# Causal attention inside a two-layer block: head pairs on 32-row quarters, values as weights on four 32-column quarters

## The reference, cut to what matters

```python
# causal attention of layer 1, per batch of 512 tokens
qkv = (x @ Wqkv).reshape(b, t, 3, H, HD)          # H = 8 heads, HD = 16
scores = q @ k.T * scale + head_scales * geo_bias # the bias is folded into Wqkv's q part
scores = where(causal, scores, -inf)
attn = softmax(scores)
out = attn @ v                                    # then @ Wout, times the gate, + x
```

## Time and profile before

| what | value |
|---|---|
| median of 3 runs (2993.34 to 3004.03) | 2995.16 us |
| the profiled execution | 2994.33 us |
| its span, first to last instruction | 2992.5 us |
| mean granted TensorE clock | 0.929 of full speed |
| PE / DVE / ACT / POOL busy | 84% / 52% / 46% / 27% |
| scores of the causal attention (L888), start of the first 128-key and of the first 512-key one, batch alone | 195.4 and 228.6 us |
| the same, first batch beside running heads | 449.1 and 496.2 us |
| starts of that block in the next five batches | 797.9, 1149.4, 1501.8, 1852.5, 2200.7 us |

### The profile page before, as it was taken

The page is one execution under the profiler, slowest core; times in us unless marked ns, Lnnn a source line. Parts: engine busy times, 40 slices in busy tenths (PEclk is TensorE's granted clock), DMA queues, the critical chain, the costliest instruction groups (busy, mean ns, idle before and its releaser), DMA issues. The chain is left out here.

```text
span 2992.5 us, 45343 instructions
## 1 busy us (share of the span) xinstructions
PE 2503.9 (84%) x15660; PEld 1542.3 (52%) x15660; DVE 1556.1 (52%) x2640; ACT 1361.7 (46%) x2923; POOL 802.5 (27%) x376
## 2 busy tenths in 40 slices
PE   4886899889897898889898898978988898976676
PEld 2354347544565546654465445754456544753454
DVE  4224673547536483455735475364834557347432
ACT  0232236462455525563364624645255633643354
POOL 1001650018301290014600174011910147015200
PEclk6886899999899998999899998999989999998798
DMA  2110110103010120112101030101201121000111
GB/s 76 42 50 1 33 39 8 51 15 89 2 43 15 43 62 2 43 29 57 34 1 57 15 79 12 43 15 43 61 2 43 29 57 33 15 19 15 23 29 33
DMA packets 210740, 101.70 MB, mean 34 GB/s; under 512 B 137367, under 2 KB 189620, under 8 KB 210492
## 3 DMA queue, kind: packets, MB, share of 16 engines
q1 hardware_dynamic: 205052, 95.74, 11.4%
q10 hardware_dynamic: 5440, 2.75, 0.3%
HBM read 77.48 MB, written 20.99 MB: 33 GB/s over the span
## 5 line engine op out<-in xcount | busy, mean ns | idle before, releaser
L721 POOL TENSOR_TENSOR prod<-pv,mixv 128x1024 f32<-128x1024 f32 x190 | 610.5, 3257 | 251.9 <-ACT pv L1179 172.7
L1561 DVE TENSOR_REDUCE nmax<-bank 128x1 f32<-128x512 f32 x512 | 341.1, 687 | 595.2 <-PE bank L1015 592.8
L1218 ACT ACTIVATE prT<-bank 128x512 f32<-128x512 f32 x512 | 305.7, 597 | 624.5 <-PE bank L736 620.9
L1015 PE MATMUL bank<-keys,qs 64*128 64x512 f32 x896 | 279.6, 702 | 191.6 <-ACT pr L1231 61.5
L660 POOL TENSOR_TENSOR rstd<-vareps,minus_half 128x4 f32<-128x4 f32 x48 | 48.5, 1010 | 1288.7 <-DVE vareps L1325 1288.7
L1231 ACT ACTIVATE pr<-bank,nmax 128x512 f32<-128x512 f32 x512 | 349.9, 686 | 82.4 <-DVE nmax L1561 81.0
L736 PE MATMUL bank<-ident,pr 128*128 128x128 f32 x2048 | 353.5, 299 | 35.5 <-ACT prT L1218 35.5
L736 PEld LDWEIGHTS bank<-ident,pr 128*128 128x128 f32 x2048 | 243.2, 151 | 269.2 <-issue 216.6
L1119 ACT ACTIVATE arena<-bank 128x512 f32<-128x512 f32 x256 | 152.9, 597 | 473.0 <-PE bank L848 423.0
L1052 PE MATMUL bank<-prT,vals 128*64 128x128 f32 x3584 | 264.5, 293 | 47.5 <-ACT prT L1218 47.5
L1523 DVE TENSOR_REDUCE vals<-prod 128x128 f32<-128x1024 f32 x224 | 269.3, 1209 | 42.5 <-POOL prod L721 42.5
(11 more groups left out here) (231 smaller groups left out, 3274.2 us busy)
## 6 DMA issues: line engine op xcount, KB each, us to landing
Wg<-in_L_ffn_Wg SPq DMA_DIRECT2D x64, 256.0 KB, 2.7
Wu<-in_L_ffn_Wu SPq DMA_DIRECT2D x64, 256.0 KB, 3.1
Wd<-in_L_ffn_Wd SPq DMA_DIRECT2D x64, 256.0 KB, 3.8
out_rows<-on SPq DMA_DIRECT2D x32, 512.0 KB, 2.6
onR<-out_rows SPq DMA_DIRECT2D x32, 512.0 KB, 3.8
xin<-in_L_attn_x SPq DMA_DIRECT2D x8, 256.0 KB, 4.0
mask_rows<-masko SPq DMA_DIRECT2D x8, 256.0 KB, 4.3
maskR<-mask_rows SPq DMA_DIRECT2D x8, 256.0 KB, 6.6
```

The costliest lines, as they stand in the source:

```text
L721: g.tensor_tensor(*value_piece(n), ALU.mult).then_inc(vprod_r[0], 1)
L1015: pe.matmul((S0, S1)[(turn + odd) % 2][:, :], qs[half, j % 3, r, :], keys[half, p, :], start=True, stop=True).then_inc(s_ps[0], 1)
L1218: s.activation(prT[:, m % 3, :], TB[:, :], ACT.Copy).then_inc(pT_r[0], 1)
L1561: v.tensor_reduce(nmax[:, m % 2:m % 2 + 1], (S0, S1)[turn % 2][:, :], X_AXIS, ALU.max, negate=True).then_inc(nmax_r[0], 1)
```

## The change

The causal attention's matmuls are cut to tiles of the array, and what is weight and what is streamed is swapped in the value product.

- Masked keys: instead of eight copies, `k1z` has two (`[2, T]`): heads of even number kept, or heads of odd number kept. DVE makes both straight from PSUM. The copies on ACT and POOL are gone.
- Scores: two heads of a pair are issued together at even steps, each on its own 32 rows of the array (a 32-row quarter holds an even and an odd head; the mask of the copy blanks the other). The order of heads is `ORDER1`, so that a pair lies on two different quarters. Both wait for the exp of the head before, because both banks F0 and F2 are written.
- `p1` has four buffers, `p1T` six, `nmax1` four columns.
- Value product: `v1` (padded to 32 columns) is the weight on one of four 32-column quarters, `p1T` is streamed, four heads (`QUAD`) at a time at steps n % 4 == 2. It comes out transposed, ACT copies it to `o1T`, two transposes bring it back, and DVE copies as before.
- The stage has two more marks (`E1`).

```diff
-E1 = A1 + N1 + 3
+E1 = A1 + N1 + 5
+ORDER1 = (0, 2, 1, 3, 4, 6, 5, 7)
+QUAD = 4
+DV = 32
+NPT = 6
...
-        k1z = part(0, [H1, T])
-        v1 = sb("v1", [P, NT, H1, D1 + 1])
-        nmax1 = sb("nmax1", [P, 2])
-        p1 = part(4096, [2, T])
-        p1T = part(5120, [2, T])
+        k1z = part(0, [2, T])
+        v1 = sb("v1", [P, NT, H1, DV])
+        o1T = sb("o1T", [P, 2 * P])
+        nmax1 = sb("nmax1", [P, 4])
+        p1 = part(1024, [4, T])
+        p1T = part(3072, [NPT, T])
...
-                wait(g, k1_r, b, 1)
-                for h in range(H1 // 2, H1):
-                    g.tensor_tensor(k1z[:, h, :], k1T, head_of16[:, h:h + 1].to_broadcast([P, T]), ALU.mult).then_inc(k1z_r[1][0], 1)
...
-                for n in range(N1 + 3):
-                    if n < N1:
-                        i, h = n // H1, n % H1
+                wait(pe, k1_r, b, 2)
+                for n in range(N1 + 5):
+                    if n < N1 and n % 2 == 0:
+                        i = n // H1
                         w = (i + 1) * P
-                        f = (F0, F2)[n % 2]
-                        if i == 0:
-                            wait(pe, k1z_r[h // (H1 // 2)], b, h % (H1 // 2) + 1)
-                        if n >= 2:
-                            wait(pe, p1_r, b, n - 1)
-                        pe.matmul(f[:, 0:w], q1T[:, i * P:(i + 1) * P], k1z[:, h, 0:w], start=True, stop=False, skip_group_check=True)
-                        pe.matmul(f[:, w - P:w], ident_bf[:, :], causal_bf[:, :], start=False, stop=True, skip_group_check=True).then_inc(s1_ps[0], 1)
+                        wait(pe, p1_r, b, n)
+                        for odd, f in enumerate((F0, F2)):
+                            h = ORDER1[n % H1 + odd]
+                            rows = slice(h // 2 * 2 * D1, h // 2 * 2 * D1 + 2 * D1)
+                            pe.matmul(f[:, 0:w], q1T[rows, i * P:(i + 1) * P], k1z[rows, h % 2, 0:w], start=True, stop=False, skip_group_check=True)
+                        for f in (F0, F2):
+                            pe.matmul(f[:, w - P:w], ident_bf[:, :], causal_bf[:, :], start=False, stop=True, skip_group_check=True).then_inc(s1_ps[0], 1)
...
-                    if n >= 3:
+                    if 3 <= n <= N1 + 2 and n % QUAD == (QUAD + 2) % QUAD:
...
                         for j in range(i + 1):
-                            last = pe.matmul(F1[:, h * (D1 + 1):(h + 1) * (D1 + 1)], p1T[:, m % 2, j * P:(j + 1) * P], v1[:, j, h, :], start=(j == 0), stop=(j == i))
+                            for k in range(QUAD):
+                                h = ORDER1[QUAD * half + k]
+                                c = h % QUAD * DV
+                                last = pe.matmul(F1[c:c + DV, half * P:(half + 1) * P], v1[:, j, h, :], p1T[:, (m - QUAD + 1 + k) % NPT, j * P:(j + 1) * P], start=(j == 0), stop=(j == i), skip_group_check=True)
...
+                    if n >= H1 + 4 and n % H1 == 4:
+                        i = n // H1 - 1
+                        wait(pe, o1T_r, b, i + 1)
+                        for half in range(2):
+                            last = pe.transpose(F1[:, (2 + half) * P:(3 + half) * P], o1T[:, half * P:(half + 1) * P], ident[:, :])
+                        last.then_inc(o1_ps[0], 1)
...
-                for h in range(H1 // 2):
-                    s.activation(k1z[:, h, :], k1T, ACT.Copy, scale=head_of16[:, h:h + 1]).then_inc(k1z_r[0][0], 1)
...
+                    if n >= H1 + 3 and n % H1 == 3:
+                        i = n // H1 - 1
+                        wait(s, o1T_ps, b, 2 * i + 2)
+                        s.activation(o1T[:, :], F1[:, 0:2 * P], ACT.Copy).then_inc(o1T_r[0], 1)
...
-                v.tensor_copy(k1T, F2[:, :]).then_inc(k1_r[0], 1)
+                for odd in range(2):
+                    v.tensor_scalar(k1z[:, odd, :], F2[:, :], parity[:, odd:odd + 1], None, ALU.mult).then_inc(k1_r[0], 1)
```

More of the change, by code:

```diff
@@ L359, in build @@
         p1T_r = sem("p1T_r", N1)
+        o1T_ps = sem("o1T_ps", 2 * NT)
+        o1T_r = sem("o1T_r", NT)
         o1_ps = sem("o1_ps", NT)
@@ L895, in attn1 @@
                             wait(pe, p1T_r, b, m)
-                        transposes(F3, lambda j: p1[:, m % 2, j * P:(j + 1) * P], i + 1).then_inc(p1_T[0], 1)
-                    if n >= 3:
+                        transposes(F3, lambda j: p1[:, m % 4, j * P:(j + 1) * P], i + 1).then_inc(p1_T[0], 1)
+                    if 3 <= n <= N1 + 2 and n % QUAD == (QUAD + 2) % QUAD:
                         m = n - 3
-                        i, h = m // H1, m % H1
-                        if h == 0 and i >= 1:
+                        i, half = m // H1, m % H1 // QUAD
+                        if half == 0 and i >= 1:
                             wait(pe, o1_r, b, i)
@@ L1140, in attn1 @@
                         wait(s, p1_T, b, m + 1)
-                        s.activation(p1T[:, m % 2, 0:w], F3[:, 0:w], ACT.Copy).then_inc(p1T_r[0], 1)
+                        if m >= NPT:
+                            wait(s, o1T_ps, b, (m - NPT) // QUAD + 1)
+                        s.activation(p1T[:, m % NPT, 0:w], F3[:, 0:w], ACT.Copy).then_inc(p1T_r[0], 1)
                     if n < N1:
@@ L1144, in attn1 @@
                         wait(s, nmax1_r, b, n + 1)
-                        if n >= 2:
-                            wait(s, p1_T, b, n - 1)
-                        s.activation(p1[:, n % 2, 0:w], (F0, F2)[n % 2][:, 0:w], ACT.Exp, bias=nmax1[:, n % 2:n % 2 + 1]).then_inc(p1_r[0], 1)
+                        if n >= 4:
+                            wait(s, p1_T, b, n - 3)
+                        s.activation(p1[:, n % 4, 0:w], (F0, F2)[n % 2][:, 0:w], ACT.Exp, bias=nmax1[:, n % 4:n % 4 + 1]).then_inc(p1_r[0], 1)
                     yield A1 + 1 + n
@@ L1429, in attn1 @@
                 wait(v, qkv1_ps, b, 2)
-                v.tensor_copy(k1T, F2[:, :]).then_inc(k1_r[0], 1)
+                for odd in range(2):
+                    v.tensor_scalar(k1z[:, odd, :], F2[:, :], parity[:, odd:odd + 1], None, ALU.mult).then_inc(k1_r[0], 1)
                 yield A1
-                for n in range(N1 + 3):
-                    if n >= H1 + 3 and n % H1 == 3:
+                back = F1[:, 2 * P:4 * P].rearrange("p (h e) -> p h e", e=DV)[:, :, 0:D1 + 1]
+                for n in range(N1 + 5):
+                    if n >= H1 + 5 and n % H1 == 5:
                         i = n // H1 - 1
                         wait(v, o1_ps, b, i + 1)
-                        v.tensor_copy(o1[:, i, :, :].rearrange("p h d -> p (h d)"), F1[:, 0:H1 * (D1 + 1)]).then_inc(o1_r[0], 1)
+                        v.tensor_copy(o1[:, i, :, :], back).then_inc(o1_r[0], 1)
                     if n < N1:
@@ L1439, in attn1 @@
                         wait(v, s1_ps, b, n + 1)
-                        if n >= 2:
-                            wait(v, p1_r, b, n - 1)
-                        v.tensor_reduce(nmax1[:, n % 2:n % 2 + 1], (F0, F2)[n % 2][:, 0:w], X_AXIS, ALU.max, negate=True).then_inc(nmax1_r[0], 1)
+                        if n >= 4:
+                            wait(v, p1_r, b, n - 3)
+                        v.tensor_reduce(nmax1[:, n % 4:n % 4 + 1], (F0, F2)[n % 2][:, 0:w], X_AXIS, ALU.max, negate=True).then_inc(nmax1_r[0], 1)
                     yield A1 + 1 + n
                 wait(v, o1_ps, b, NT)
-                v.tensor_copy(o1[:, NT - 1, :, :].rearrange("p h d -> p (h d)"), F1[:, 0:H1 * (D1 + 1)]).then_inc(o1_r[0], 1)
+                v.tensor_copy(o1[:, NT - 1, :, :], back).then_inc(o1_r[0], 1)
                 wait(v, o1_r, b, NT)
```

15 lines of the change are left out of this document (7 added, 8 removed).

## The result

The change takes 3080.18 us (median of 4 runs, 3070.89 to 3081.10) against 2994.25 (4 runs, 2988.66 to 3004.03): ratio 1.0279, interval 1.0258 to 1.0299. That is 86 us slower where 13 were predicted, and outside the range. The profiled execution has a span of 3078.7 us.

What follows compares the result with a forecast made beforehand. TensorE was taken to bound the causal-attention block. 2994.3 us plus 3.5 for seven batches beside running heads (+0.5 each) plus 9 for the batch alone gave 3007 us; 8-in-10 range 2960 to 3050.

Steps and rivals of the forecast that it cites:

- PE's saving, 12.7 us a batch: Causal attention's tiled scores and value products take 32.3 us of PE per batch instead of 45.0, saving 12.7.
- that rival: Value products: four column tiles overlap only two by two, 4.4 us more per batch, 3042 us; chance 0.10.
- Masked keys, 1.7 us: Dropping ACT's masked key copies lets the running head's max and exp start earlier: 1.7 us gained per batch.
- New waits, 15.8 us more a batch: Score pairs beside running heads wait longer, mainly for exps: 18.8 us per batch, replacing 3.0 of old waits.
- "I take +0.5" a batch: Net per batch beside running heads: sum +1.4, lowered to +0.5 because waits were charged in full; 3.5 us for seven.
- The two more marks: Two more steps at the end of the stage, priced in the batch alone: about 1.3 us.
- The batch alone, +9: The batch without running heads gets slower: pairs +6.4, end steps 1.3, copies -1.5, clock 0 to 8; +9 in all.
- the clock's term: In the batch alone, PE about half busy lowers the granted clock: 0 to 8 us more.
- My check for this batch: The batch alone should take 57 to 68 us in the next profile instead of 53.
- The slower rival: Running heads' copies and exps delay odd heads' exps on ACT at most pairs: 3041 us, range 3021 to 3075; chance 0.22.

Runs made afterwards that it cites:

- products: Kernel before with the change's column-tiled value products, head order and two marks; whole-array single scores and eight key copies as before: 2977.39 us, ratio 0.9928.
- order: The change with transposes, products and transposes back written ahead of the score pair in each step, same instructions: 3051.12 us, ratio 1.0186.
- pair: The change with its score pairs on the whole array and eight masked key copies instead of 32-row tiles and two copies: 3111.96 us, ratio 1.0377.
- spread: The change with only its table of weights altered, so a running-head step stands ahead of each pair: 2921.38 us, ratio 0.9728.
- filler: The change plus ten unread mask products on PE ahead of 10 of the 15 later score pairs per batch: 3051.05 us, ratio 1.0183.
- spread, filler: The spread kernel plus ten unread mask products ahead of 10 of the 15 later score pairs, in the batch alone only: 2913.13 us, ratio 0.9738.

## Why the prediction was wrong, point by point

- **PE's saving, 12.7 us a batch: right in kind, 2.3 too small.** It is 15.0 by the account. A quad of value products shows 32 instructions from 507.21 to a modelled end 1.08 us later (*products*), eight waves of 0.11 and 0.20 around them, so four column tiles overlap as two do and that rival falls. Two 32-row scores start 0.007 us apart.
- **Masked keys, 1.7 us: right.** The 2.77 us wait of the earlier trace rows is 1.00 us, and two copies instead of eight gave 15 us in all.
- **New waits, 15.8 us more a batch: right.** 14.9 by the account, 17.1 instead of 3.0 in the profile's list of the block, L1162 as releaser. `o1T`'s copy releases nobody for long, and the transposes back do not stand in that list.
- **"I take +0.5" a batch: the step that failed.** I let PE's rate stand at full clock through seven blocks that I had just filled with waits, and charged the clock (0 to 8 us) only to the batch alone. It cost 13.0 us a batch, 11.7 of them inside the block. From the second batch's first score to the last batch's, six batches on, the program takes 2093.2 us before and 2167.6 after, +74.4 where I had +3.0; this is nearly all of the error of 73. Not all of the loss is the new waits': 2.8 of the 11.7 us come with the two marks alone, and pairs on the whole array lose 5.7 less than the same pairs on row tiles. The row that should have warned was mine: the clock of 0.57 in a stretch where PE was half busy.
- **The two more marks.** I priced them only where the batch stands alone (1.3 us). Beside running heads they alone cost 22 us in all, mostly through the clock (+4.0 us a batch).
- **The batch alone, +9: too small.** Its first score to the next batch's went from 253.7 to 269.7 us, +16. I had the clock's term at about 3 us; it is 14.6. My check for this batch was missed too: its last value products start 70.5 us after its first score (195.8 to 266.3), where I had 57 to 68.
- **The slower rival** had the right sign and almost the right time (3041, to 3075), but not the mechanism: ScalarE's queue was to decide from an average wait of 1.11 us at the 15 pairs, and the waits were 12.9 us for those pairs, 0.86 each.
- **Open:** why *order* lost so much less to the clock in the block than the change (4.0 against 12.8 us) with nearly the same waits (14.7 and 17.1). That where a wait stands counts, not only its length, is argued and not shown. Waits and row tiles together cost more clock than each alone adds (9.1 against 3.4 and 1.9 us); why is open too.

## What to carry to other kernels

Price a change in three columns: work at full clock, waits, and what the waits do to the clock under all the work around them, also work that you don't touch. A longer hand-over isn't a reason to drop a cheaper form: give the order something to put into it, and change the order's table together with the kernel, since marks that were only added cost 22 us and a new table gave 159. When a gain is missing, try each half by itself, in the old order and in the new one; the tables above read differently by column.

## What the runs showed of the hardware

- **Row tiles and the clock.** In the batch alone (197 to 242 us) all eight versions with 32-row scores and no filler were granted 0.50 to 0.56, and all ten with whole-array scores 0.73 to 0.96. PE's busy time does not tell them apart: 42.64 of 45 us at 0.52, 31.02 at 0.81 (*pair*). Beside running heads it depends on the order: in the tight table pairs on row tiles lose 12.8 us in the block and pairs on the whole array 7.1, while *spread* loses 0.0 there with the same row tiles (13.1 in the whole batch, before 14.8).
- **One list, two clocks.** The same list of instructions was granted 0.92 (*filler*) and 0.58 (*spread, filler*) from 197 to 242 us, though both ran at full clock and in step until 196.8. What decides it isn't settled here, so a difference in granted clock between two single stretches proves little; the eight against ten above carry weight because none is on the wrong side.
- **A lone row tile** is no cheaper and costs 0.19 us more than the whole array at 384 keys (0.84 against 0.65 us to the next matmul). The Trainium skill ("TensorEngine Tiling (Array Packing)", Key Properties) says that changing the tiling mode drains the engine. This trace fits that; how much of the 0.19 us is the drain no run here splits off.
